# Self-attention of sixteen short sequences: scores three pairs ahead, and half of the last rotation behind the first division

## The chip, the core and the metric

The kernel runs on one core of a Trainium2 chip. The metric is the device time of one execution in microseconds (us). Its engines have names of their own in the profile: PE is TensorE (matrix products; PEld its weight loads), DVE is VectorE, ACT is ScalarE, POOL is GpSimd, SP is SyncE, which issues the transfers. Each engine takes its instructions in the order of the program and waits at semaphores for the others.

## What is computed

Four transformer-like blocks in a row over x (16 sequences of 56 tokens, 256 features) with a context of 1500 tokens per sequence. The change touches only the self-attention at the start of the first block:

```
x = rms_norm(hidden_states, ln_in_w)
mixed = jnp.where(vm, x @ v_qkv, x @ l_qkv)
q, k, v = jnp.split(mixed, 3, axis=-1)
q, k, v = (heads(q, NH, HD), heads(k, NH, HD), heads(v, NH, HD))
q, k = apply_rotary(q, k, position_ids, l)
ctx = sdpa(q, k, v, causal=True)          # 16 heads of 16 features, 56 x 56 scores, softmax
ctx = ctx.transpose(0, 2, 1, 3).reshape(b, l, H)
attn_out = jnp.where(vm, ctx @ v_dense, ctx @ l_dense)
hidden_states = residual + attn_out
```

`apply_rotary` gives `q * cos + rotate_half(q) * sin`, and the same for k. Behind it stand the cross-attentions and feed-forward layers, which take over 90% of the time and are the same in both kernels.

## The kernel before

Features lie on the partitions, the 896 tokens along the free axis, in two halves of 448 (`half(h)`), that is 8 sequences each. `R` holds q, k and v as six tiles `qkv[:, m]` of 128 features: m = 0, 1 are q, 2, 3 are k, 4, 5 are v.

**Rotation.** For each half and each of the four tiles of q and k (in the order `TURNED` = 2, 3, 0, 1), TensorE makes the turned copy (`turn`, one product with a constant), and VectorE's `rotate(h, m)` does three instructions of 448 columns: the sine product out of PSUM into XN (L1359), which also frees the PSUM bank; the cosine product in place (L1360); their sum in place (L1362), which raises the semaphore `rotated`. The last two tiles of the second half (m = 0, 1: its q) are rotated in the middle of the first pair, ahead of the first division.

**Pairs.** Self-attention works on two sequences at a time, a pair i of `HB` = 8. Nearly all tiles are there twice and are taken in turns (`i % 2`). For a pair:

- staging: ScalarE's `sa_stage` spreads v (L909, two instructions) and q (L912); GpSimd's `stage_keys` makes k masked by head (L697, four products);
- TensorE `sa_scores`: in two banks the causal mask (L1877) and q times k (L1879);
- VectorE `sa_maximum` (L1371) and `sa_shift`, which subtracts the maximum out of PSUM (L1377);
- ScalarE `sa_exps` (L917);
- VectorE `sa_total` (the sum L1382, its reciprocal L1385) and `sa_divide` (L1389), which gives the probabilities;
- TensorE `sa_turned`: eight transposes of the probabilities into banks 1 and 2 (line 1902 in the rows); ScalarE `sa_turned` copies them to SBUF (L937, two instructions);
- TensorE `sa_values`: v transposed into bank 0 (L1891 in the rows); ScalarE `sa_values` copies it out (L927, two);
- TensorE `sa_attended`: probabilities times values into bank 3 (L1916); ScalarE `sa_attended` copies the result to XN (L944).

Each engine's order is written out by hand as a loop over i. TensorE runs attended(i-1), values(i+1), scores(i+2), turned(i). ScalarE runs stage(i+2), attended(i-1), values(i+1), exps(i+1), turned(i). VectorE runs maximum(i+1), total(i), shift(i+1), divide(i). GpSimd makes the keys of pair i as soon as scores(i-2) are done. Keys of pair 4 and later also wait until the second half's k is rotated, and the staging of pair 4 until all of `rotated` is there. Behind the last pair follow the split of XN by expert on VectorE (L1273, L1276) and the dense product on TensorE (L1810).

Of the kernel before, what the change touches and what calls it, by code (L numbers as in the profile page):

```python
# [40 lines left out]
HT = T // 2  # L41
# [157 lines left out]
def build(nc, a, out):  # L199

    ctx = ExitStack()
    with ctx:
# [648 lines left out]
        def _(act):  # L851
# [97 lines left out]
            sa_stage(1)  # L949
            sa_exps(0)  # L950
            sa_values(0)
            for i in range(HB):
                if i + 2 < HB:
                    sa_stage(i + 2)
                if i > 0:
                    sa_attended(i - 1)
                if i + 1 < HB:
                    sa_values(i + 1)
                    sa_exps(i + 1)
                sa_turned(i)  # L960
            sa_attended(HB - 1)

# [257 lines left out]
        def _(dve):  # L1220
# [131 lines left out]
            def rotate(h, m):  # L1352

                src = take(dve, ("turn", h, m))
                if turns[0] > 0:
                    dve.wait_ge(sem("rotated"), turns[0])
                turns[0] += 1
                other, own = XN[:, m % 2, half(h)], qkv[:, m, half(h)]
                inc_empty(V.tensor_tensor(by_seq(other), by_seq(src[:, 0:HT]), bs(sinT), ALU.mult))  # L1359
                then(V.tensor_tensor(by_seq(own), by_seq(own), bs(cosT), ALU.mult))  # L1360
                emptied(dve, ("turn", h, m))
                V.tensor_tensor(own, own, other, ALU.add).then_inc(sem("rotated"), 1)  # L1362
# [28 lines left out]
            for name, m in SECOND_HALF:  # L1391
# [4 lines left out]
                if name == "turn":  # L1396
                    rotate(0, m)
                else:
                    leave(1, m)
# [12 lines left out]
            for m in TURNED[0:2]:  # L1412
                rotate(1, m)
            for i in range(HB):
                if i + 1 < HB:
# [4 lines left out]
                if i == 0:  # L1420
                    for m in TURNED[2:4]:
                        rotate(1, m)
                sa_divide(i)
            for h in range(2):
                dve.wait_ge(sem("sa_out"), HB // 2 * (h + 1))
                by_expert("experts2", h)
# [368 lines left out]
        def _(pe):  # L1795
# [138 lines left out]
            for m in TURNED[2:4]:  # L1934
                turn(1, m)
            sa_values(0)
            for i in range(HB):
                if i > 0:
                    sa_attended(i - 1)
                if i + 1 < HB:  # L1940
                    sa_values(i + 1)
                if i + 2 < HB:
                    sa_scores(i + 2)
                sa_turned(i)
            sa_attended(HB - 1)

# [586 lines left out]
```

## Time and profile before

| | |
|---|---|
| time, median of 3 runs | 1597.53 us (1596.61 to 1602.24) |
| the profiled execution, its own time | 1597.96 us |
| its span in the profile | 1596.2 us |
| mean granted TensorE clock | 0.98 of full |
| TensorE busy | 1476.0 us, 92% of the span |
| VectorE busy | 945.8 us, 59% |
| ScalarE busy | 621.8 us, 39% |
| GpSimd busy | 539.6 us, 34% |
| DMA engines, hardware queue | 17.7% of 16 engines' span |

The span goes from the first to the last instruction; the execution's own time has 1.8 us around it. Busy shares are averages over very different stages. Self-attention of the pairs lies between about 66 and 120 us. A timeline row gives start, duration, engine, line, operation, what is written and read, how often it stands in a row, and in square brackets how long the engine was idle before it and who ended that.

### The profile page before, as it was taken

The numbers are of one execution on the slowest core, as the hardware profiler recorded it, in microseconds if no ns is written. First come the engines' busy times: TensorE is split into PE (matmuls) and PEld (weight loads), VectorE is DVE, ScalarE is ACT, GpSimd is POOL, SyncE is SP. The second block draws the span as 40 slices with busy tenths as digits, with TensorE's granted clock in tenths as the row PEclk, the third lists the DMA queues.
The fourth block names the chain that finished last, engine by engine and source line by source line (L and its number), as shares of the span: only waits on it lengthen the run. The fifth ranks groups of instructions, "written<-read, shape, count | busy, mean of one in ns | idle before, by whom it ended". The sixth has DMA issues, their size and how long they took to land.

```text
span 1596.2 us, 21925 instructions
## 1 busy us (share of the span) xinstructions
PE 1476.0 (92%) x8042; PEld 781.9 (49%) x8043; DVE 945.8 (59%) x1605; ACT 621.8 (39%) x1014; POOL 539.6 (34%) x425
## 2 busy tenths in 40 slices
PE   6779999999999899989988899999999889999898
PEld 3346555555555444446654344455344344555344
DVE  6877666666666264114437677777333768778440
ACT  1253466666666520035542233334122333333131
POOL 1620488888888910000001133332000133333000
PEclk9989999999999999989999999999999989999999
DMA  7001532232331140023212001110031001110000
GB/s 253 0 2 36 136 97 71 76 98 64 84 80 50 27 138 0 0 78 106 88 34 64 0 25 43 40 36 1 2 112 65 0 21 40 36 36 13 2 0 23
DMA packets 42276, 82.96 MB, mean 52 GB/s; under 512 B 6252, under 2 KB 28188, under 8 KB 42156
## 3 DMA queue, kind: packets, MB, share of 16 engines
q1 hardware_dynamic: 42160, 81.48, 17.7%
q8 instruction: 65, 1.06, 0.3%
q14 instruction: 51, 0.42, 0.1%
HBM read 59.31 MB, written 0.97 MB: 38 GB/s over the span
## 4 chain that ended last, share of the span: by engine, by line
PE 79%; DVE 12%; POOL 3%; ACT 2%; issue 2%; DMA 0%; SPq 0%; POOLq 0%; ACTq 0%; DVEq 0%
PE psum L1810 21%; PE psum L2393 8%; PE psum L2051 5%; PE psum L2027 5%; PE psum L2001 3%; PE psum L2334 3%; DVE WBZ L1713 3%; PE psum L1984 3%; PE psum L2201 3%; PE psum L1970 2%; POOL XN L780 2%; PE psum L2365 2%; DVE WA L1453 2%; PE psum L2401 2%; PE psum L2385 2%
## 5 line engine op out<-in xcount | busy, mean ns | idle before, releaser
L1453 DVE TENSOR_REDUCE WA<-psum 112x2 f32<-112x1000 f32 x192 | 229.8, 1201 | 89.9 <-PE psum L2001 89.9
L780 POOL TENSOR_TENSOR XN<-XN,WBZ 125x896 f32<-125x896 f32 x128 | 266.5, 2082 | 16.8 <-POOL XN L780 0.9
L1172 ACT ACTIVATE WA<-psum,y_bias 125x448 f32<-125x448 f32 x192 | 121.1, 633 | 227.7 <-PE psum L2388 226.7
L1006 ACT ACTIVATE WBZ<-psum 125x896 f32<-125x896 f32 x192 | 175.5, 915 | 43.9 <-PE psum L2027 33.3
L2393 PE MATMUL psum<-WA,ctxN 125*128 125x448 f32 x384 | 179.8, 552 | 0.4 <-ACT WA L1172 0.4
L812 POOL TENSOR_TENSOR XN<-const,y_max 112x896 bf16<-112x896 f32 x32 | 53.7, 1679 | 309.6 <-DVE y_max L1700 237.4
L1700 DVE CUSTOM_DVE_ANT_0 XA<-psum,WA 112x375 bf16<-112x375 f32 x240 | 122.7, 540 | 35.9 <-PE psum L2365 35.9
L803 POOL TENSOR_SCALAR ctxT<-ctxT 128x375 f32<-128x375 f32 x32 | 56.1, 1754 | 190.3 <-ACT std L881 187.8
L2027 PE MATMUL psum<-R 100*125 100x224 f16 x768 | 110.6, 266 | 0.0
L1713 DVE RECIPROCAL WBZ<-WBZ 128x224 f32<-128x224 f32 x68 | 105.2, 1549 | 1.2
L2365 PE MATMUL psum<-XB,R 128*112 128x375 f16 x240 | 77.7, 344 | 22.7 <-DVE y_max L1700 22.7
L2027 PEld LDWEIGHTS psum<-R 100*125 100x125 f16 x768 | 78.9, 135 | 28.3 <-issue 25.0
L1810 PE MATMUL psum<-R,WBZ 128*128 128x448 f32 x224 | 88.5, 548 | 2.5 <-ACT R L886 2.5
L2393 PEld LDWEIGHTS psum<-WA,ctxN 125*128 125x128 f32 x384 | 67.3, 191 | 31.7 <-ACT WA L1172 24.4
L2001 PE MATMUL psum<-WA,XB 32*112 32x500 f16 x384 | 79.3, 413 | 2.5 <-DVE WA L1453 2.3
L1810 PE MATMUL psum<-XA,WA 64*128 64x448 f32 (+1 forms) x216 | 72.5, 573 | 2.1 <-DVE XA L1634 2.0
L2385 PE MATMUL psum<-R,XB 128*125 128x448 f16 x192 | 68.7, 358 | 4.9 <-POOL XN L812 4.9
L2365 PEld LDWEIGHTS psum<-XB,R 128*112 128x112 f16 x240 | 31.6, 131 | 84.3 <-DVE y_max L1700 69.5
L2388 PE MATMUL psum<-XN,minusb 112*125 112x448 bf16 x192 | 68.9, 359 | 0.0
L2387 PE MATMUL psum<-R,XB 128*125 128x448 f16 x192 | 68.5, 357 | 0.0
L2386 PE MATMUL psum<-R,XB 128*125 128x448 f16 x192 | 68.4, 356 | 0.0
L1810 PEld LDWEIGHTS psum<-R,WBZ 128*128 128x128 f32 x224 | 40.9, 189 | 50.1 <-issue 44.7
(266 smaller groups left out, 2567.4 us busy)
## 6 DMA issues: line engine op xcount, KB each, us to landing
R<-WA SPq DMA_DIRECT2D x192, 93.8 KB, 2.2
ctxT<-in_ctxT SPq DMA_DIRECT2D x12, 750.0 KB, 4.2
R<-in_ctxT SPq DMA_DIRECT2D x12, 750.0 KB, 5.4
WA<-in_ctxT SPq DMA_DIRECT2D x8, 750.0 KB, 4.2
ctxT<-in_ctxT SPq DMA_DIRECT2D x32, 187.5 KB
ctxN<-in_ctx SPq DMA_DIRECT2D x32, 187.5 KB
WBZ<-in_x_w SPq DMA_DIRECT2D x4, 1024.0 KB, 6.3
WA<-bias_rows SPq DMA_DIRECT2D x30, 82.0 KB, 3.8
```

The lines of the kernel that those rows point to most:

```text
L780: nc.gpsimd.tensor_tensor(z_sum[b % 2][0:TK, :], first[0:TK, :], z_p[t % 4][0:TK, :], ALU.add)\
L1006: nc.scalar.activation(z_p[t % 4][0:TK, :].rearrange("p (k n) -> p k n", k=2), psum[0:TK, s:s + 2, 0:2 * GC], ACT.Exp, scale=float(CHD0) * ...
L1172: nc.scalar.activation(y_pT[t][0:TK, g * HALF:(g + 1) * HALF], bank[2 + u % 3][0:TK, 0:HALF], ACT.Exp, bias=y_bias[0:TK, bass.ds(b * NT + ...
L1453: V.tensor_reduce(z_mx[0:PR, r:r + 3:2, c], psum[0:PR, lo:lo + 2, 0:PC], AX_X, ALU.max)\
L1700: V.tensor_tensor_reduce(y_masked[0:PR, j % 2, 0:CK], bank[j % 2][0:PR, 0:CK], y_mask[0:PR, s, 0:CK], 1.0, -3e38, ALU.add, ALU.max, y_max[ ...
L1713: V.reciprocal(part, part).then_inc(sem("x2_inverted"), 1)
L1810: mm = pe.matmul(bank[bk][0:w.shape[-1], 0:HT], w, m, start=(i == 0), stop=(i == len(parts) - 1))
L2001: mm = pe.matmul(bank[lo + j][0:PR, 0:PC], z_dh[at, b, 2 * (i % 2):2 * (i % 2) + 2, :].rearrange("p h s -> p (h s)"), z_kh[b % 2][at, c * ...
L2027: mm = pe.matmul(bank[2 * (t % 2) + g // 2][0:TK, g % 2 * GC:(g % 2 + 1) * GC], KS[0:KR, b % 2, g, t * TK:(t + 1) * TK], QS[0:KR, g, b, :] ...
L2365: return pe.matmul(bank[j % 2][0:PR, 0:CK], y_q[:, b, 0, j * PR:(j + 1) * PR], y_k[:, s, 0, 0:CK], start=True, stop=True)
L2385: pe.matmul(dst, y_k[:, s, 0, at], q[0], start=True, stop=False)
L2393: return pe.matmul(bank[5 + g][:, 0:HALF], ctxN[s][0:TK, t, :], y_pT[t][0:TK, g * HALF:(g + 1) * HALF], start=(t == 0), stop=(t == KT - 1))
```

## The change

Three of the hand-written orders change; no instruction is added or removed.

- TensorE: scores run three pairs ahead instead of two, and stand between turned(i) and attended(i). values(i+2) follow attended(i). Scores of pair 2 stand ahead of values of pair 1.
- ScalarE: the loop is values(i+1), turned(i), exps(i+2), attended(i), stage(i+4); staging of pairs 2 and 3 and the exponential of pair 1 stand ahead of the loop.
- VectorE: `rotate` is cut in two. The sine product stays in it, the cosine product and the sum are `rotated`. For the last two tiles `rotated` comes behind the division of pair 0. The wait of the sine product on the semaphore `rotated` asks for one less.

```diff
             sa_stage(0)
             sa_stage(1)
             sa_exps(0)
+            sa_stage(2)
             sa_values(0)
+            sa_exps(1)
+            sa_stage(3)
             for i in range(HB):
-                if i + 2 < HB:
-                    sa_stage(i + 2)
-                if i > 0:
-                    sa_attended(i - 1)
                 if i + 1 < HB:
                     sa_values(i + 1)
-                    sa_exps(i + 1)
                 sa_turned(i)
-            sa_attended(HB - 1)
+                if i + 2 < HB:
+                    sa_exps(i + 2)
+                sa_attended(i)
+                if i + 4 < HB:
+                    sa_stage(i + 4)
...
             def rotate(h, m):
 
                 src = take(dve, ("turn", h, m))
-                if turns[0] > 0:
-                    dve.wait_ge(sem("rotated"), turns[0])
+                if turns[0] > 1:
+                    dve.wait_ge(sem("rotated"), turns[0] - 1)
                 turns[0] += 1
+                other = XN[:, m % 2, half(h)]
+                inc_empty(V.tensor_tensor(by_seq(other), by_seq(src[:, 0:HT]), bs(sinT), ALU.mult))
+
+            def rotated(h, m):
                 other, own = XN[:, m % 2, half(h)], qkv[:, m, half(h)]
-                inc_empty(V.tensor_tensor(by_seq(other), by_seq(src[:, 0:HT]), bs(sinT), ALU.mult))
                 then(V.tensor_tensor(by_seq(own), by_seq(own), bs(cosT), ALU.mult))
                 emptied(dve, ("turn", h, m))
                 V.tensor_tensor(own, own, other, ALU.add).then_inc(sem("rotated"), 1)
...
                     for m in TURNED[2:4]:
                         rotate(1, m)
                 sa_divide(i)
+                if i == 0:
+                    for m in TURNED[2:4]:
+                        rotated(1, m)
...
             sa_values(0)
+            sa_scores(2)
+            sa_values(1)
             for i in range(HB):
-                if i > 0:
-                    sa_attended(i - 1)
-                if i + 1 < HB:
-                    sa_values(i + 1)
+                sa_turned(i)
+                if i + 3 < HB:
+                    sa_scores(i + 3)
+                sa_attended(i)
                 if i + 2 < HB:
-                    sa_scores(i + 2)
-                sa_turned(i)
-            sa_attended(HB - 1)
+                    sa_values(i + 2)
```

The lines of the changed kernel are shifted: on VectorE by up to 5, on TensorE by 10.

TensorE in the middle of the pairs, before: L1902 are the turned probabilities, L1916 attended values, L1891 values, L1877 and L1879 scores.

```order
L1902 MATMUL psum<-const,WBZ 128x128 x8
L1916 MATMUL psum<-WBZ 32x56 x16
L1891 MATMUL psum<-const,R 128x128 x4
L1877 MATMUL psum<-probs 128x448
L1879 MATMUL psum<-R 64x448 x2
L1877 MATMUL psum<-probs 128x448
L1879 MATMUL psum<-R 64x448 x2
L1902 MATMUL psum<-const,R 128x128 x8
```

The same place after, where L1912, L1926, L1901, L1887 and L1889 are those lines.

```order
L1912 MATMUL psum<-const,R 128x128 x8
L1887 MATMUL psum<-probs 128x448
L1889 MATMUL psum<-R 64x448 x2
L1887 MATMUL psum<-probs 128x448
L1889 MATMUL psum<-R 64x448 x2
L1926 MATMUL psum<-R 32x56 x16
L1901 MATMUL psum<-const,R 128x128 x4
L1912 MATMUL psum<-const,WBZ 128x128 x8
```

The scores moved from behind attended and values to between turned and attended.

VectorE from the subtraction of pair 1 to the maximum of pair 2, before: L1359, L1360 and L1362 are the rotation, L1389 is the division.

```order
L1377 TENSOR_TENSOR WBZ<-psum,small 128x16x56
L1359 TENSOR_TENSOR XN<-psum,sinT 128x448
L1360 TENSOR_TENSOR R<-R,cosT 128x448
L1362 TENSOR_TENSOR R<-R,XN 128x448
L1359 TENSOR_TENSOR XN<-psum,sinT 128x448
L1360 TENSOR_TENSOR R<-R,cosT 128x448
L1362 TENSOR_TENSOR R<-R,XN 128x448
L1389 TENSOR_TENSOR R<-R,nmax 128x16x56
L1371 TENSOR_REDUCE small<-psum 128x16
```

And after, where L1361, L1365, L1367 and L1394 are those lines.

```order
L1382 TENSOR_TENSOR WBZ<-psum,small 128x16x56
L1361 TENSOR_TENSOR XN<-psum,sinT 128x448 x2
L1394 TENSOR_TENSOR R<-R,nmax 128x16x56
L1365 TENSOR_TENSOR R<-R,cosT 128x448
L1367 TENSOR_TENSOR R<-R,XN 128x448
L1365 TENSOR_TENSOR R<-R,cosT 128x448
L1367 TENSOR_TENSOR R<-R,XN 128x448
L1376 TENSOR_REDUCE small<-psum 128x16
```

The division stands four instructions earlier; the maximum of pair 2 has the same work ahead of it.

ScalarE in the loop, after: L927 values, L937 the copy of the turned probabilities, L917 the exponential of the pair after next, L944 attended, L909 and L912 staging. Before, L937 was followed at once by L909 and L912 of the pair after next, and L917 was the last ahead of L937.

```order
L927 ACTIVATE R<-psum 64x16x16 x2
L937 ACTIVATE WBZ<-psum 128x512 x2
L917 ACTIVATE WBZ<-WBZ 128x16x56
L944 ACTIVATE XN<-psum 128x2x112
L909 ACTIVATE R<-R 128x2x2x56 x2
L912 ACTIVATE R<-R 128x2x2x56
```

The staging moved behind the exponential and the attended values.

## Rows read from the trace of the kernel before

**Rows 1.** The page: TensorE's busy time, and the chain by engine.

```profile
PE 1476.0 (92%) x8042; PEld 781.9 (49%) x8043; DVE 945.8 (59%) x1605; ACT 621.8 (39%) x1014; POOL 539.6 (34%) x425
...
PE 79%; DVE 12%; POOL 3%; ACT 2%; issue 2%; DMA 0%; SPq 0%; POOLq 0%; ACTq 0%; DVEq 0%
```

**Rows 2.** TensorE's timeline, 66 to 85 us: start, duration, engine, line, operation.

```profile
68.92 0.35 PE L1877 MATMUL psum<-probs 128*128 128x448 bf16 x1 [0.36 <-issue]
...
70.40 0.97 PE L1879 MATMUL psum<-R 128*64 128x448 f32 x4
76.33 1.97 PE L1902 MATMUL psum<-const,R 128*128 128x128 f32 x8 [4.96 <-DVE R L1389]
```

**Rows 3.** TensorE's timeline over one pair, 84.9 to 92 us.

```profile
84.97 1.09 PE L1902 MATMUL psum<-const,WBZ 128*128 128x128 f32 x8
87.24 0.60 PE L1916 MATMUL psum<-WBZ 128*32 128x56 f32 x32 [1.17 <-ACT WBZ L937]
...
90.65 1.09 PE L1902 MATMUL psum<-const,R 128*128 128x128 f32 x8
```

**Rows 4.** VectorE's timeline, 52 to 137 us.

```profile
70.18 0.61 DVE L1359 TENSOR_TENSOR XN<-psum,sinT 128x448 f32<-128x448 f32 x1
70.71 0.62 DVE L1360 TENSOR_TENSOR R<-R,cosT 128x448 f32<-128x448 f32 x1
...
73.30 1.24 DVE L1362 TENSOR_TENSOR R<-R,XN 128x448 f32<-128x448 f32 x1
74.46 1.82 DVE L1389 TENSOR_TENSOR R<-R,nmax 128x896 f32<-128x896 f32 x1
76.20 1.08 DVE L1371 TENSOR_REDUCE small<-psum 128x16 f32<-128x896 f32 x1
...
79.73 1.08 DVE L1389 TENSOR_TENSOR WBZ<-WBZ,nmax 128x896 f32<-128x896 f32 x1
85.09 1.09 DVE L1371 TENSOR_REDUCE small<-psum 128x16 f32<-128x896 f32 x1 [4.28 <-PE psum L1879]
```

**Rows 5.** GpSimd's timeline: two products of pair 4, four of pair 5.

```profile
71.53 1.25 POOL L697 TENSOR_TENSOR R<-R,const 128x448 f32<-128x448 f32 x1 [2.22 <-PE psum L1879]
...
74.02 1.31 POOL L697 TENSOR_TENSOR R<-R,const 128x448 f32<-128x448 f32 x1
...
85.14 3.62 POOL L697 TENSOR_TENSOR R<-R,const 128x448 f32<-128x448 f32 x4 [8.06 <-PE psum L1879]
```

**Rows 6.** ScalarE's timeline, 84.9 to 92 us.

```profile
86.10 1.08 ACT L937 ACTIVATE WBZ<-psum 128x512 f32<-128x512 f32 x2 [2.83 <-PE psum L1902]
87.07 0.67 ACT L909 ACTIVATE R<-R 128x224 f32<-128x224 f32 x2
87.63 0.39 ACT L912 ACTIVATE R<-R 128x224 f32<-128x224 f32 x1
```

**Rows 7.** Stretches: us, PE, PEld, DVE, ACT, POOL busy, clock, DMA, GB/s.

```profile
80.00:84.20 4.20, 4.20 (x32) 1.71 (x26) 0.81 (x1) 2.32 (x5) 0.00 (x0) 0.50 0.02 4
...
90.00:95.70 5.70, 4.53 (x56) 2.28 (x54) 4.52 (x5) 3.90 (x10) 3.62 (x4) 1.00 0.00 1
...
111.50:114.90 3.40, 1.26 (x20) 1.02 (x24) 2.80 (x4) 2.46 (x5) 0.00 (x0) 1.00 0.00 0
```

**Rows 8.** TensorE's timeline, 107 to 124 us: the tail, the dense products.

```profile
107.67 1.09 PE L1902 MATMUL psum<-const,WBZ 128*128 128x128 f32 x8
...
112.47 1.09 PE L1902 MATMUL psum<-const,R 128*128 128x128 f32 x8 [1.34 <-DVE R L1389]
...
115.53 1.97 PE L1902 MATMUL psum<-const,WBZ 128*128 128x128 f32 x8
118.68 0.97 PE L1916 MATMUL psum<-WBZ 128*32 128x56 f32 x32 [1.17 <-ACT WBZ L937]
119.58 2.83 PE L1810 MATMUL psum<-XA,WA 128*128 128x448 f32 x4
122.25 1.67 PE L1810 MATMUL psum<-XB,WA 128*128 128x448 f32 x4
```

More of the change, by code:

```diff
@@ L1397, in _ @@
                     rotate(0, m)
+                    rotated(0, m)
                 else:
@@ L1423, in _ @@
                 sa_divide(i)
+                if i == 0:
+                    for m in TURNED[2:4]:
+                        rotated(1, m)
             for h in range(2):
```

## The prediction

> **What bounds the kernel now.** The page first: TensorE is busy 92% of the span, and 79% of the chain that ended last runs through it, so time is won only where TensorE waits [rows 1]. The change touches self-attention alone, about 66 to 120 us. There I read TensorE's timeline for its gaps, then the other engines' for what fills them. Three kinds of gap show. One of 4.96 us before the first turned probabilities (76.33) ends with VectorE's first division [rows 2]. In every pair, 1.18 us pass between turned probabilities and attended values, while ScalarE copies the transposes out of PSUM: 84.97 + 1.09 = 86.06 to 87.24 [rows 3]. And a tail: pairs 6 and 7 have nothing to put in between [rows 8]. A pair costs 90.65 - 84.97 = 5.68 us, which is turned 1.09, the gap 1.18, and 3.41 for attended, values and scores (87.24 to 90.65) [rows 3]. VectorE needs 79.73 + 1.08 - 76.20 = 4.61 us for a pair [rows 4], and it idles for TensorE's scores (4.28 us before 85.09) [rows 4]. So TensorE's own order sets the pace.
>
> **Part 1, the start.** Row 68.92: scores of pair 2 wait for ScalarE's staging, which stood behind a 0.77 us copy of values; now it stands ahead of it. They start at about 68.1 and end at 70.6 instead of 71.4 [rows 2]. GpSimd's four key products, released by them, start at 70.7 instead of 71.53 [rows 5]. VectorE issues the two sine products at 70.18 and 70.71 (0.53 us is the spacing of the first two of rows 4) and reaches the first division at 71.25. There is contention in the rows: an instruction of 448 elements that reads two SBUF tensors takes 0.62 us alone (70.71) and 1.24 beside GpSimd's product (73.30), the division 1.08 alone (79.73) and 1.82 beside it (74.46), and GpSimd's product, 0.9 alone (four in 3.62), goes to 1.31 [rows 4, 5]. The division now waits until GpSimd's first product ends at 71.65 and ends itself at 72.65. **Turned probabilities of pair 0 start at 72.7 instead of 76.33**, 3.6 us earlier.
>
> **Part 2, what the early division leaves late.** The four other rotation instructions (cosine product and sum, twice) come behind it. They run beside GpSimd's remaining three products and the first of the next four. Row 73.30 to row 74.46 is 1.16 us for such an instruction under contention. Low bound: no contention, 4 x 0.58 = 2.3 us. High bound: all four contended and in line with their predecessors, 4 x 1.25 = 5.0. I take 4 x 1.2 = 4.8, since each meets a product in progress. So the maximum of pair 2 starts at 72.65 + 4.8 = 77.5 instead of 76.20, and the division of pair 1 ends at 77.5 + 4.61 = 82.1. **Turned probabilities of pair 1 start at 82.15 instead of 84.97**, 2.8 us earlier: 0.8 of the 3.6 is lost here again.
>
> The Trainium skill, SBUF - State Buffer, section "SBUF: two separate sides", has a rule that speaks against this part: a VectorE instruction with two SBUF inputs and a GpSimd one that reads SBUF lock each other out for a whole instruction. By that rule alone five VectorE instructions (the division, four of the rotation) would each stand behind up to one full product, 5 x 0.9 = 4.5 us at most, where the rows give what I use, 0.4 + 2.5 = 2.9; the sum would be up to 1.6 us longer. The trace agrees in kind: the measured excess is 0.6 and 0.7 us.
>
> **Part 3, the clock.** TensorE now runs turned 0, scores 3, attended 0 and values 2 from 72.7: 1.09 + 3.41 = 4.5 us, to 77.2; the copy between is covered. Then it has nothing until 82.15, 4.95 us. In a gap of 4.96 us before, the granted clock went to half (1.2 of 2.4 GHz), and it came back at 84.2, 7.9 us after TensorE resumed; the last 4.2 of them were without a pause [rows 2, 7]. I expect the fall again. How long it lasts after 82.15 is bounded by 4.2 (no pause now, the scores fill the copy's gap) and 7.9; I take 5.5, near the lower end for that reason. Half clock for 5.5 us costs 2.75 us of work. **Turned 2 starts at 82.15 + 4.5 + 2.75 = 89.4** instead of 90.65.
>
> **Part 4, the steady pairs.** The copy's gap is gone: turned, scores, attended, values make 5.68 - 1.18 = 4.5 us. Who is late next? VectorE, 4.61, but it is ahead of TensorE after part 3. ScalarE: busy 3.9 us in a pair [rows 7]. Its queue has one new wait: the exponential of pair i+2 stands before the staging of pair i+4 and waits for VectorE's subtraction. Staging takes 1.0 us (87.07 to 87.63 + 0.39) [rows 6] from the end of values on TensorE, which turned (1.09) just covers; so scores are held by 0.1 us at most. The copies themselves, 1.08, now lie beside scores of 2.4. GpSimd's 3.6 us per pair lies beside all of it [rows 5]. Turned 3, 4, 5: 89.4 + 3 x 4.5 = **102.9 instead of 107.67** [rows 8].
>
> **Part 5, the tail.** VectorE's maximum of pair 4 waits for scores 4, which end at 82.15 + 1.09 + 2.4 + 2.75 = 88.4 (2.4 for scores is 68.92 to 70.40 + 0.97 in rows 2). From there four pairs of 4.61 bring the division of pair 6 to 106.8, later than TensorE is free: 102.9 + 2.27 for turned and the bare copy, + 1.0 for attended and values (3.41 less 2.4), is 106.2. Turned 6 at 106.85 instead of 112.47. Then nothing covers the copies: attended 6 at 109.1, turned 7 at 109.7, attended 7 at 111.95, and the **dense product starts at 112.5 instead of 119.58** [rows 8]: 7.1 us. Before, the clock was at half there, and the first dense product took 2.83 us instead of 1.67 [rows 8], 1.16 more. If the clock is up there now, this comes on top.
>
> **Sum.** 7.1 + 1.1 = 8.2 us. Behind it everything follows at a fixed distance: TensorE runs without pause from 119.58 on, and the chain of the whole span has no transfer in it (DMA 0% in rows 1). The profiled execution took 1597.96 us (span 1596.2), 0.4 over the median, so 1589.8 for its like and 1597.53 - 8.2 = **1589.3** for the median.
>
> **Rivals.** *(a) The clock falls in the tail as well.* For: it fell before turned 7, where TensorE had worked 1.26 us between 111.5 and 114.9 [rows 7]; the bare copies of the tail stay. Against: the gap of 1.34 us before turned 6 [rows 8], where TensorE waited for VectorE, shrinks to 0.7, so the tail is denser. Price: what it cost before, turned 7 with 1.97 instead of 1.09, attended 7 with 0.97 instead of 0.60, and 1.16 in the dense product, 2.4 in all: 5.8 us, **1591.7**.
>
> *(b) The start is better.* The clock holds, or GpSimd's products don't meet the rotation. Without the low clock VectorE sets the pace: division 6 ends at 82.1 + 5 x 4.61 = 105.2, 1.6 us earlier: **1587.7**; without contention as well, 2.5 more: 1585.2. For: nothing but that a gap's place against the clock's changes may differ. Against: both showed in the rows of before.
>
> *(c) ScalarE's new wait binds.* If its exponential holds back the staging in each steady pair by 0.5 us, four pairs make 2 us: **1591.3**. Against: 3.9 us of work in 4.5, so ScalarE has 0.6 to spare.
>
> *(d) The head start is given back* at the first start of the cross-attention, by a load or by GpSimd: **1597.5**. Against: the two contexts and the weights are loaded from the start of the program, and what waits for the last attended values (two loads of SyncE's queue) has the whole dense stage beside it.
>
> *(e) Slower than before: the clock stays low.* With a gap of 5 us and then a tail, TensorE could stay at 1.2 GHz through all pairs. A pair then costs 9.0 us instead of 5.68; turned 5 at 82.15 + 4 x 9.0 = 118.2 instead of 107.67, 10.5 later, about 1 more behind it: **1609**. It decides from the point where the low stretch lasts 16 us more than I assume (16 / 2 = 8 us, the whole gain). Against: it came back each time that TensorE had work without pause.
>
> **How the numbers follow.** The forecast 0.40, (a) 0.25, (b) 0.17, (c) 0.08, (d) 0.04, (e) 0.06. The size of the forecast's own unknowns (contention 2.3 to 5.0, low clock 4.2 to 7.9 us) is worth from -3.1 (2.5 and half of 1.3) to +1.4 us (0.2 and half of 2.4). A measurement of this kernel tells about 0.5% from no change, 8.0 us, 1589.5: the forecast stands right on it. Of its own 0.40 I count 0.23 beyond 0.5%, of (a) and (c) 0.05, of (b) all: faster 0.45, within 0.5% 0.49, slower 0.06. The range reaches from the better half of (b) to beyond (a) and (c): 1586 to 1594.5; left out are (d), (e) and the best of (b).
>
> **What would show it.** Right: turned 0 near 72.7, a gap of 5 us before turned 1 near 82, half clock for 4 to 8 us behind it, then 4.5 us between turned probabilities, no wait of TensorE for the PSUM copy in pairs 0 to 4, and the dense product at 112.5 with 1.67 us. Wrong: turned 1 before 80 (no contention), pairs of 5 us or more with TensorE waiting for ScalarE's staging (c), or a wait at the start of the cross-attention that was not there (d).

## The result, and the profile after

The changed kernel took **1591.19 us** (median of 6 runs, 1590.39 to 1592.23) against 1601.12 of the kernel before (median of 6, 1596.61 to 1602.24). The ratio is 0.9945 with a 95% interval of 0.993 to 0.9959 (the two medians alone would give 0.9938): faster, by about half a percent. The profiled executions went from 1597.96 to 1590.39, their spans from 1596.2 to 1588.6 us. The kernel before does not always take the same time: its runs beside the experiments lie near 1597, near 1602 and near 1612 to 1617 us, each group at a lower mean clock (0.980, 0.975, 0.967), and what probably makes the highest group is shown under "Rotated later". Profiles are therefore compared here by the stretch of this one stage.

The page of the kernel after: busy times, and shares of the chain that ended last by engine.

```profile
PE 1473.9 (93%) x8042; PEld 780.1 (49%) x8043; DVE 946.9 (60%) x1605; ACT 621.6 (39%) x1014; POOL 539.5 (34%) x425
...
PE 79%; DVE 13%; POOL 3%; issue 2%; ACT 2%; DMA 0%; SPq 0%; POOLq 0%; ACTq 0%; DVEq 0%
```

Nothing changed in what bounds the kernel; only idle time of TensorE went. Its timeline after (start, duration, engine, line, operation, operands, idle before), to be laid beside [rows 2, 3, 8]. L1912 are the turned probabilities of pairs 0, 1, 2, 3, 5, 6 and 7, L1887 the first scores of pair 5, L1926 the last attended values, L1820 the dense product:

```profile
72.15 1.09 PE L1912 MATMUL psum<-const,R 128*128 128x128 f32 x8 [1.51 <-DVE R L1394]
...
81.79 1.97 PE L1912 MATMUL psum<-const,WBZ 128*128 128x128 f32 x8 [5.14 <-DVE WBZ L1394]
...
88.67 1.04 PE L1912 MATMUL psum<-const,R 128*128 128x128 f32 x8
89.92 0.35 PE L1887 MATMUL psum<-probs 128*128 128x448 bf16 x1 [0.21 <-issue]
...
93.33 1.04 PE L1912 MATMUL psum<-const,WBZ 128*128 128x128 f32 x8
...
102.64 1.04 PE L1912 MATMUL psum<-const,WBZ 128*128 128x128 f32 x8
...
106.41 1.09 PE L1912 MATMUL psum<-const,R 128*128 128x128 f32 x8 [0.38 <-DVE R L1394]
...
109.21 1.09 PE L1912 MATMUL psum<-const,WBZ 128*128 128x128 f32 x8
111.48 0.98 PE L1926 MATMUL psum<-WBZ 128*32 128x56 f32 x32 [1.18 <-ACT WBZ L937]
112.38 2.86 PE L1820 MATMUL psum<-XA,WA 128*128 128x448 f32 x4
```

The gap of 4.96 us before turned 0 [rows 2] is 1.51 now, and one of 5.14 stands before turned 1. Pairs follow at 4.66 us (88.67 to 93.33) instead of 5.68 [rows 3]. The dense product starts at 112.38 instead of 119.58 [rows 8], and takes 2.86 us as it took 2.83: it lies at half clock again. Stretches of the same kernel, with the granted clock (PEclk) to be compared with [rows 7]:

```profile
core 0: us, PE busy (x) PEld busy (x) DVE busy (x) ACT busy (x) POOL busy (x), PEclk, DMA share, GB/s
...
80.50:87.30 6.80, 5.51 (x18) 2.40 (x18) 5.66 (x7) 4.71 (x10) 0.00 (x0) 0.50 0.00 0
...
111.20:114.60 3.40, 3.12 (x35) 1.93 (x36) 1.66 (x3) 0.58 (x2) 0.00 (x0) 0.50 0.28 47
```

**Where the 7.6 us of the span are.** TensorE reaches this stage a little earlier or later in every execution, for reasons ahead of the change. So I count from the start of the last turned copy of q and k (one group of four products, 64.84 before, 64.31 after), called *offset* from here on:

```profile
64.84 1.77 PE L1810 MATMUL psum<-R,const 128*128 128x448 f32 x4
```
```profile
64.31 1.77 PE L1820 MATMUL psum<-R,const 128*128 128x448 f32 x4
```

The kernel after was 0.53 earlier there by chance. Turned 2 came at an offset of 24.36 instead of 25.81: 1.45 gained. From turned 2 to the dense product it took 23.71 instead of 28.93: 5.22 gained. The dense product's offset is thus 48.07 instead of 54.74, 6.67 less, and that of the end of its first four products 50.93 instead of 57.57. The other 0.4 lies in all the rest of the span. Of the 7.6 us, then, 6.6 to 6.7 are the change's in this pair of profiles, and 1.0 is chance.

### The profile page after: what moved, and what is told of

The parts are those of the page before. It is cut to its first block, busy times and chain, and to the rows that moved or that the text cites. A ratio compares the mean times of both kernels' runs of the same rounds, so it can differ in the third digit from the quotient of the medians.

```text
span 1588.6 us, 21924 instructions
## 1 busy us (share of the span) xinstructions
PE 1473.9 (93%) x8042; PEld 780.1 (49%) x8043; DVE 946.9 (60%) x1605; ACT 621.6 (39%) x1014; POOL 539.5 (34%) x425
## 4 chain that ended last, share of the span: by engine, by line
PE 79%; DVE 13%; POOL 3%; issue 2%; ACT 2%; DMA 0%; SPq 0%; POOLq 0%; ACTq 0%; DVEq 0%
PE psum L1820 21%; PE psum L2403 8%; PE psum L2061 5%; PE psum L2037 5%; PE psum L2011 4%; PE psum L2344 3%; DVE WBZ L1723 3%; PE psum L1994 3%; PE psum L2211 3%; PE psum L1980 2%; POOL XN L780 2%; PE psum L2375 2%; DVE WA L1463 2%; PE psum L2411 2%; PE psum L2395 2%
## 5 line engine op out<-in xcount | busy, mean ns | idle before, releaser
L1820 PE MATMUL psum<-R,WBZ 128*128 128x448 f32 x224 | 88.5, 548 | 2.5 <-ACT R L886 2.5
L1820 PE MATMUL psum<-XA,WA 64*128 64x448 f32 (+1 forms) x216 | 72.5, 573 | 2.1 <-DVE XA L1644 1.9
L1820 PEld LDWEIGHTS psum<-R,WBZ 128*128 128x128 f32 x224 | 40.9, 189 | 50.1 <-issue 44.7
```

What stands on the lines that cost most here:

```text
L1820: mm = pe.matmul(bank[bk][0:w.shape[-1], 0:HT], w, m, start=(i == 0), stop=(i == len(parts) - 1))
```

## The experiments

Each kernel is given as a difference from the changed kernel. "Dense" is the dense product's offset, "first product" that of the end of its first four products; before 54.74 and 57.57, after 48.07 and 50.93. Times without an interval are one execution each. A ratio is taken against the runs of the kernel before that were made beside the kernel in question. The share of its high runs differs between these sets (above 1611 us: 0 of 6, 5 of 18, 6 of 19 and 1 of 19), and for the same changed kernel the ratio is 0.9945 in one set and 0.9906 in another; so ratios of different sets should not be compared closely. All offsets are of one profile each, and where the half clock falls differs between profiles of one kernel: the changed kernel, profiled again (below), has 46.68 and 48.45. Differences of some 2.5 us in the stage can be due to that.

**Orders only.** The whole rotation stands ahead of the division again; the orders of TensorE and ScalarE are the changed ones.

```diff
                     for m in TURNED[2:4]:
                         rotate(1, m)
+                        rotated(1, m)
                 sa_divide(i)
-                if i == 0:
-                    for m in TURNED[2:4]:
-                        rotated(1, m)
```

> The new orders of TensorE and ScalarE, with VectorE's rotation whole and ahead of the first division as before. My theory is that the start is worth little, because what the early division wins is lost to the contention with GpSimd, the gap before the second turned probabilities and the low clock behind it, and that the gain comes from the pairs: turned 0 at about 76, no gap before turned 1 (which starts at about 83, TensorE being the late one), turned 5 at about 102 and the dense product at 112 to 113 as in the changed kernel (112.4), so about 8 us less than the kernel before. The rival: the 3.6 us at the start are kept, so that without them the dense product starts at about 116 and the gain is 4 to 5 us.

Measured 1591.54 us (9 runs, 1583.03 to 1604.3), ratio 0.9923 (0.9876 to 0.9969); dense 46.81, first product 48.58: in the stage this is 1.3 us less than the first profile of the full change and 0.1 more than its second, so the split shows no gain of its own here. TensorE's rows, turned 0, 1, 2 and the dense product:

```profile
77.07 1.97 PE L1910 MATMUL psum<-const,R 128*128 128x128 f32 x8 [5.58 <-DVE R L1394]
...
83.91 1.04 PE L1910 MATMUL psum<-const,WBZ 128*128 128x128 f32 x8
...
88.63 1.04 PE L1910 MATMUL psum<-const,R 128*128 128x128 f32 x8
...
111.96 1.77 PE L1818 MATMUL psum<-XA,WA 128*128 128x448 f32 x4
```

By offset turned 0 is 4.1 us later than after (11.92 against 7.84), and the gap of 5.6 stands before it. But the half clock (75.7 to 82.5) then lies under turned 0 and scores 3, VectorE's division 1 is done meanwhile (at 81.54, where turned 1 starts at 83.91), and turned 1 waits for nothing. Turned 2 is at an offset of 23.48, 0.9 ahead of the first profile of the full change (24.36) and 0.1 behind its second (23.35). The split only moves the gap, and the half clock with it, from before turned 0 to before turned 1.

**Vector only.** The split rotation alone; TensorE's and ScalarE's loops are those of before. Only TensorE's part of the edit is shown.

```diff
...
             sa_values(0)
-            sa_scores(2)
-            sa_values(1)
             for i in range(HB):
-                sa_turned(i)
-                if i + 3 < HB:
-                    sa_scores(i + 3)
-                sa_attended(i)
-                if i + 2 < HB:
-                    sa_values(i + 2)
+                if i > 0:
+                    sa_attended(i - 1)
+                if i + 1 < HB:
+                    sa_values(i + 1)
+                if i + 2 < HB:
+                    sa_scores(i + 2)
+                sa_turned(i)
+            sa_attended(HB - 1)
...
```

> Only VectorE's part of the change: half of the last rotation behind the first division, the orders of TensorE and ScalarE as before. My theory: turned 0 at about 72.5, turned 1 at about 82 after a gap of about 4 us, then 5.7 us per pair as before; 0 to 3 us less than the kernel before, depending on whether the clock falls in that gap. The rival (the start is the gain): 3.5 us less or more.

Measured 1600.5 us, ratio 0.9988 (0.9959 to 1.0018): no difference. Dense 55.92, 1.2 later than before. Turned 1 and 2:

```profile
82.42 1.97 PE L1910 MATMUL psum<-const,WBZ 128*128 128x128 f32 x8 [2.93 <-DVE WBZ L1392]
...
91.71 1.09 PE L1910 MATMUL psum<-const,R 128*128 128x128 f32 x8
```

Turned 1 is 2.5 us earlier than at 84.97 [rows 3], as predicted; but half clock lasts from 81.4 to 91.6, and turned 2 is later than 90.65. Here the head start was lost to the clock that fell behind it.

**TensorE's order alone**, with ScalarE's loop and the rotation of before. Only ScalarE's loop is shown.

```diff
...
+                if i + 2 < HB:
+                    sa_stage(i + 2)
+                if i > 0:
+                    sa_attended(i - 1)
                 if i + 1 < HB:
                     sa_values(i + 1)
+                    sa_exps(i + 1)
                 sa_turned(i)
-                if i + 2 < HB:
-                    sa_exps(i + 2)
-                sa_attended(i)
-                if i + 4 < HB:
-                    sa_stage(i + 4)
+            sa_attended(HB - 1)
...
```

> Only TensorE's order of the change, ScalarE's and VectorE's as before. Scores of the third pair ahead then wait for their staging, which stands behind the copy of the turned probabilities on ScalarE: a pair should take 1.1 + 1.1 + 1.0 + 2.4 + 0.5 + 0.5 = 6.6 us instead of 5.7, and the kernel be 3 to 4 us slower than before. If TensorE's order were enough, a pair would take 4.5 to 4.7 us as in the changed kernel.

Measured 1632.13 us, dense 70.91, far more than the 3 to 4 us that I expected. Turned 1, first scores of pair 4, turned 2:

```profile
85.51 1.04 PE L1908 MATMUL psum<-const,WBZ 128*128 128x128 f32 x8
89.49 0.35 PE L1883 MATMUL psum<-probs 128*128 128x448 bf16 x1 [2.95 <-issue]
...
92.90 1.04 PE L1908 MATMUL psum<-const,R 128*128 128x128 f32 x8
```

Scores wait 2.95 us in each pair for a staging that stands behind the copy of the turned probabilities on ScalarE. A pair takes 7.39 us, and with a wait of that length in each the clock fell again and again: pairs of 8.9 and 10.1 follow. The stage is 16.2 us longer than before (70.91 against 54.74). The rest of the loss lies in the cross-attention, where half clock lasted 41 us with TensorE busy almost all the time (compare "Rotated later"):

```profile
190.30:231.30 41.00, 40.61 (x216) 20.73 (x214) 16.63 (x16) 14.55 (x18) 18.67 (x9) 0.50 0.30 80
```

TensorE's new order is a loss without ScalarE's; ScalarE's alone was not run.

**Keys late.** GpSimd's first key products of the second half wait for the whole rotation, so nothing of it runs beside the division.

```diff
-                    pool.wait_ge(sem("rotated"), 2 * KD * h + 2)
+                    pool.wait_ge(sem("rotated"), 2 * KD * h + (4 if h else 2))
```

> The changed kernel, but GpSimd's key products of pair 4 wait until all rotations are done, so they don't run beside them. If contention costs what I put down, the division takes 1.08 instead of 1.58 us, the four instructions behind it 2.4 instead of 5.1, turned 1 starts at about 79 instead of 81.8, and the gap before it is about 2 us, so that the clock may stay up; the dense product then starts at about 108 (clock up) or 109.5 (clock down). If contention does not matter, turned 1 stays at 81.8 and the dense product at 112.4, or comes later because the keys do.

Measured 1588.15 us, dense 45.26. VectorE and GpSimd in the kernel after (division 0, the first of the four rotation instructions, maximum 2; the first four key products):

```profile
70.51 1.58 DVE L1394 TENSOR_TENSOR R<-R,nmax 128x896 f32<-128x896 f32 x1
72.02 1.35 DVE L1365 TENSOR_TENSOR R<-R,cosT 128x448 f32<-128x448 f32 x1
...
77.12 1.08 DVE L1376 TENSOR_REDUCE small<-psum 128x16 f32<-128x896 f32 x1
```
```profile
70.21 5.23 POOL L697 TENSOR_TENSOR R<-R,const 128x448 f32<-128x448 f32 x4 [1.63 <-PE psum L1889]
```

and with the keys late, VectorE, then TensorE's turned 1:

```profile
71.22 1.08 DVE L1394 TENSOR_TENSOR R<-R,nmax 128x896 f32<-128x896 f32 x1
72.22 0.62 DVE L1365 TENSOR_TENSOR R<-R,cosT 128x448 f32<-128x448 f32 x1
...
74.61 1.08 DVE L1376 TENSOR_REDUCE small<-psum 128x16 f32<-128x896 f32 x1
```
```profile
79.40 1.97 PE L1912 MATMUL psum<-const,WBZ 128*128 128x128 f32 x8 [2.53 <-DVE WBZ L1394]
```

Division and rotation take 3.39 us instead of 6.61, so the contention costs VectorE 3.2. GpSimd's four products, 3.62 when undisturbed [rows 5], take 5.23 beside the division and the rotation. The gap before turned 1 halves to 2.53, yet the clock fell all the same (half from 78.7 to 85.5).

**q first.** ScalarE's staging of pair i+4 is cut in two: q ahead of the copy of the attended values, v behind it. Scores need only q; `sa_values` waits for v on a semaphore of its own. Only ScalarE's loop is shown.

```diff
...
+                if i + 4 < HB:
+                    sa_stage_q(i + 4)
                 sa_attended(i)
                 if i + 4 < HB:
-                    sa_stage(i + 4)
+                    sa_stage_v(i + 4)
...
```

> The changed kernel, but ScalarE stages q of the fourth pair ahead before it copies the attended values, with a semaphore of its own for v. In the changed kernel TensorE waits 0.21 us before the scores of each steady pair; if that is the staging of q, the wait goes and a pair takes 4.45 to 4.55 us instead of 4.66, and the dense product starts about 0.5 us earlier. If it is something else (GpSimd's keys, or the loads of weights), a pair stays at 4.66.

Measured 1589.84 us, dense 47.69. After, ScalarE's v (L909) and q (L912) end at 89.82, just ahead of the scores at 89.92:

```profile
88.87 0.67 ACT L909 ACTIVATE R<-R 128x224 f32<-128x224 f32 x2 [0.20 <-PE psum L1901]
89.45 0.37 ACT L912 ACTIVATE R<-R 128x224 f32<-128x224 f32 x1
```

With q first, turned 3, scores of pair 6, turned 4, turned 6:

```profile
92.67 1.04 PE L1935 MATMUL psum<-const,WBZ 128*128 128x128 f32 x8
93.54 0.35 PE L1909 MATMUL psum<-probs 128*128 128x448 bf16 x1
...
96.94 1.04 PE L1935 MATMUL psum<-const,R 128*128 128x128 f32 x8
...
105.76 1.09 PE L1935 MATMUL psum<-const,R 128*128 128x128 f32 x8 [1.08 <-DVE R L1416]
```

Scores start 0.87 behind turned instead of 1.25, and the pair takes 4.27. But VectorE's pace is next: turned 6 now waits 1.08 for its division instead of 0.38, and of 3 x 0.37 only 0.4 is left.

**Filled gap.** Sixteen products of constants into a free bank, 128 x 224, whose result nobody reads, stand in the gap before turned 1.

```diff
                 if i + 2 < HB:
                     sa_values(i + 2)
+                if i == 0:
+                    pe.wait_ge(sem("sa_pT"), 1)
+                    for _ in range(16):
+                        pe.matmul(bank[1][:, 0:224], mean, const[:, 0:224], start=True, stop=True)
```

> The changed kernel with 16 products without use in TensorE's gap before the turned probabilities of pair 1, so that the clock has no reason to fall there; about 4.3 us of work in a gap of 5.1. If the low clock is what makes TensorE late in pairs 1 and 2, the granted clock stays at full, turned 2 starts at about 86.4 instead of 88.7, and the dense product at about 110.5 instead of 112.4. If the clock costs nothing there, the dense product stays at 112.4.

Measured 1593.05 us, dense 46.21, 1.9 less than after; the first product ends only 1.4 earlier, as half clock came in the tail (110.1 to 116.9). The fillers and turned 1:

```profile
77.56 6.22 PE L1959 MATMUL psum<-const 128*128 128x224 f32 x32
83.62 1.04 PE L1912 MATMUL psum<-const,WBZ 128*128 128x128 f32 x8
```

They took 0.38 us each, more than the 0.27 I had counted, and delayed turned 1 by 0.8 (offset 18.23 against 17.48). Even so turned 2 came 1.85 earlier (22.51 against 24.36): the clock stayed up, and turned 1 took 1.04 instead of 1.97. That is the price of those 6.8 us of half clock by itself, 1.85 + 0.75 = 2.6 us.

**Rotated later.** The four rotation instructions stand behind the *second* division.

```diff
                 sa_divide(i)
-                if i == 0:
+                if i == 1:
                     for m in TURNED[2:4]:
                         rotated(1, m)
```

> The changed kernel with the four rotation instructions behind the division of pair 1 instead of pair 0. Turned 1 should start at about 77.3 instead of 81.8 and the gap before it go; scores of pair 4 then wait for the rotated q, to about 82.5. If the rotation's place is what costs, the maximum of pair 4 comes at about 85 instead of 87.8 and the dense product at about 110; if the wait only moves, the dense product stays at 112.

Measured 1605.63 us, with dense at 47.23, 0.8 *less* than after. Turned 1 and the first scores of pair 4:

```profile
77.04 1.09 PE L1912 MATMUL psum<-const,WBZ 128*128 128x128 f32 x8
82.61 0.53 PE L1887 MATMUL psum<-probs 128*128 128x448 bf16 x1 [4.48 <-POOL R L697]
```

The wait only moves: scores of pair 4 need keys and q of the second half. The extra 15 us are elsewhere, in the cross-attention, where half clock lasts from 166.9 to 204.4. The stretch from 166 to 204 us, first in this kernel, then in the run of the changed kernel again (below):

```profile
166.00:204.00 38.00, 37.36 (x202) 19.58 (x198) 16.07 (x16) 13.97 (x17) 18.67 (x9) 0.51 0.30 77
```
```profile
166.00:204.00 38.00, 36.61 (x350) 20.52 (x348) 25.81 (x25) 23.02 (x31) 31.90 (x19) 1.00 0.51 134
```

TensorE is busy 98% of the time, at half clock, and the view counts 202 of its instructions instead of 350. The mean clock of this execution is 0.970, and the highest times of the other kernels, the one before too, come with clocks of 0.965 to 0.971; so I take them for the same thing. No high run of the kernel before was profiled, so for that kernel it is not shown, and neither is what makes its middle group near 1602.

**All together, split rotation.** Keys late, q first, six fillers before turned 1, and three before each of the last two attended values. Only the fillers of the tail are shown.

```diff
...
                 sa_turned(i)
                 if i + 3 < HB:
                     sa_scores(i + 3)
+                if i > 5:
+                    pe.wait_ge(sem("sa_shifted"), HB)
+                    for _ in range(3):
+                        pe.matmul(bank[4][:, 0:224], mean, const[:, 0:224], start=True, stop=True)
                 sa_attended(i)
...
```

> The changed kernel with GpSimd's products of pair 4 behind the rotations, q staged ahead of the attended values' copy, six products without use in the gap before turned 1 and three in each of the two bare copies of the tail. If the three costs found add up (contention 2.8 us, low clock in the pairs 2, low clock in the tail 1.7), the clock stays at full from 65 to 130 us, VectorE sets the pace at 4.55 us a pair, turned 1 starts 14.4 us after the last turn product as in the kernel with late keys, and the first dense product ends about 44.5 us after it, where the changed kernel has 50.9: 5 to 6.5 us less than the changed kernel. If VectorE or something else takes over, less than 3 us.

Dense 42.65, first product 44.42: 6.5 less than in the first profile of the changed kernel, 4.0 less than in its second. Turned 1 and 2 and the dense product:

```profile
80.13 1.09 PE L1935 MATMUL psum<-const,WBZ 128*128 128x128 f32 x8 [0.26 <-DVE WBZ L1416]
...
84.67 1.09 PE L1935 MATMUL psum<-const,R 128*128 128x128 f32 x8
...
108.40 1.77 PE L1842 MATMUL psum<-XA,WA 128*128 128x448 f32 x4
```

The clock stays up throughout the stage, and VectorE sets the pace of 4.53. Against the first profile the costs found one at a time add up in the stage. The time doesn't show it: 1590.35 (12 runs), ratio 0.9922 (0.9885 to 0.9959). Four of the twelve runs, the profiled one among them, lie at 1603.3 to 1604.6: here half clock lasted from 161.7 to 199.2 us. The other eight have a median of 1589.4, against 1589.72 of the changed kernel in the same set.

**All together, whole rotation.** The same with the rotation of before, whole and ahead of the division, and ten fillers behind values 1 instead of the six. Only these are shown.

```diff
...
             sa_scores(2)
             sa_values(1)
+            emptied(pe, ("turn", 1, 0))
+            for _ in range(10):
+                pe.matmul(bank[1][:, 0:224], mean, const[:, 0:224], start=True, stop=True)
...
```

> The same with the rotation whole and ahead of the first division, as in the kernel before, and the products without use in the gap ahead of turned 0. If VectorE's part of the change is worth nothing, this one is within 0.5 us of the kernel with everything (turned 0 at 3 us later, turned 1 at 0.3 us later). If the early division is worth something once clock and contention are out of the way, this one is 1 us or more slower.

Measured **1584.11 us** (6 runs, 1583.13 to 1586.82), ratio 0.9866 (0.9823 to 0.9909): the best kernel of the study, and in the same set none of its runs is as slow as the fastest of the changed kernel (1588.86). Dense 43.89, first product 45.66. The fillers, turned 0, turned 1, and turned 6:

```profile
70.03 3.95 PE L1972 MATMUL psum<-const 128*128 128x224 f32 x20
73.82 1.04 PE L1933 MATMUL psum<-const,R 128*128 128x128 f32 x8
...
78.14 1.09 PE L1933 MATMUL psum<-const,WBZ 128*128 128x128 f32 x8
...
100.81 1.97 PE L1933 MATMUL psum<-const,R 128*128 128x128 f32 x8 [1.08 <-DVE R L1416]
```

With the keys late and TensorE kept at work, the whole rotation costs nothing up to the tail: turned 1 is at an offset of 14.27, where the split kernel had 14.38. In this profile the clock was at half for 3.4 us in the tail (100.4 to 103.8), under turned 6, and that is what makes dense 1.2 later than in the split kernel. Behind the first product the span is 1475.5 us long, against 1473.4 and 1473.9 in the two profiles of the changed kernel: some 1.6 to 2.1 us of what the stage gained are lost again further on. There is half clock from 527.1 to 533.9 here, which those two don't have.

**The changed kernel again**, beside the two above.

> The changed kernel again, beside the two others on the same chip: 0.993 to 0.996 of the kernel before, as measured first. In the trace, if no 35 to 40 us stretch of low clock shows in the cross-attention, the span is near 1588.6 us.

Measured 1589.72 us (8 runs), ratio 0.9906 (0.9872 to 0.9939). The last turned copy, turned 1, turned 2 and the dense product:

```profile
65.49 1.77 PE L1820 MATMUL psum<-R,const 128*128 128x448 f32 x4
...
82.96 1.97 PE L1912 MATMUL psum<-const,WBZ 128*128 128x128 f32 x8 [5.14 <-DVE WBZ L1394]
...
88.84 1.04 PE L1912 MATMUL psum<-const,R 128*128 128x128 f32 x8
...
112.17 1.77 PE L1820 MATMUL psum<-XA,WA 128*128 128x448 f32 x4
```

The same instructions give dense 46.68 and first product 48.45, 1.4 and 2.5 less than in the first profile: half clock lasted 3.4 us behind turned 1 (82.8 to 86.2) instead of 6.8 and didn't come in the tail, where the dense product's first row is 1.77 and not 2.86.

**Without fillers, whole rotation**: keys late and q first alone, the rotation of before.

```diff
...
                     for m in TURNED[2:4]:
                         rotate(1, m)
+                        rotated(1, m)
                 sa_divide(i)
-                if i == 0:
-                    for m in TURNED[2:4]:
-                        rotated(1, m)
...
```

> The orders of TensorE and ScalarE of the change, VectorE's rotation whole as before, GpSimd's products of pair 4 behind the rotations, q staged ahead; no products without use. If those only keep the clock up and cost nothing else, the gap before turned 0 (about 4 us) brings a low clock of 3.4 or 6.8 us, and the dense product starts 45 to 46.5 us after the last turn product (43.9 with them): 1.5 to 2.5 us slower than that kernel, 1586 to 1587 in executions without the long low stretch in the cross-attention. If the filling has a cost of its own further on, as the times of the kernel with everything (1589 without the long stretch) may mean, this one is as fast as it or faster.

Measured 1590.52 us (10 runs), ratio 0.9943 (0.9915 to 0.9972); dense 45.39, first product 48.46. TensorE waits 3.41 us before turned 0, and half clock came there for 3.4 us and in the tail for 10.2.

**Without fillers, split rotation**: the same two, the rotation as changed.

> The same with the rotation split as in the changed kernel. A gap of about 2.5 us before turned 1; with a low clock there the dense product starts about 45 us after the last turn product, as in the kernel with late keys (45.3) less 0.3. If the early division is worth nothing, the time is within 1 us of the kernel with the whole rotation.

Measured 1588.85 us (10 runs, of which one took 2877.33 us; no trace shows why, and the ratio leaves it out), ratio 0.9928 (0.9904 to 0.9952); dense 45.03, first product 47.99, half clock for 10.2 us in the tail. Here too split and whole rotation differ by less than can be told (0.4 us in the stage; the intervals overlap). Beside the two kernels with everything, 48.46 and 47.99 stand against 45.66 and 44.42: in the stage of these profiles the fillers are worth 2.8 and 3.6 us, by keeping the clock up. In the whole span they are worth less: behind the first product the two kernels without fillers have 1473.7 and 1473.8 us, and the one with fillers and whole rotation has 1475.5. In time (medians of all runs) the four are at 1584.1 against 1590.5 us (whole) and 1590.4 (1589.4 without its high runs) against 1588.9 (split), in two different sets of runs.

## Why the prediction was right, point by point

The forecast was 8.2 us, a ratio of 0.9949; measured were 0.9945 and 7.6 us between the two spans. The mechanism was right: turned 0 early, a gap and half clock before turned 1, then pairs without the copy's gap. As offsets, forecast and measured are 17.31 and 17.48 for turned 1, 24.56 and 24.36 for turned 2, 38.06 and 38.33 for turned 5, 47.66 and 48.07 for the dense product, 49.33 and 50.93 for the end of its first four products. Two errors cancel in the middle: from turned 1 to turned 2 I had 7.25 us where it took 6.88, and for the next three pairs 13.5 where they took 13.97.

The closeness of the totals is partly luck. The change itself gave 6.6 us at the end of the first product, 1.6 less than forecast: attended 7 at half clock cost 0.4 of that and the first dense product 1.2. The 1.0 us of chance outside the stage makes it 7.6. The time, 1591.19, lies nearer to rival (a)'s 1591.7 than to my 1589.3. And the ratio is near 0.9949 also because the kernel before came out higher in its later runs (median 1601.12 of six, where I had 1597.53 of three). The second profile of the changed kernel gained 9.1 us at the end of the first product, 0.9 more than forecast.

- **Part 1, right.** Turned 0 at 72.15 for 72.7, and 0.53 of that difference is the chance lead at the start of the stage. The contended division took 1.51 us from its start to the next (70.51 to 72.02), within the 1.0 and 1.8 that [rows 4] gave.
- **Part 2, right as a mechanism, a little short.** The four rotation instructions took 5.10 us (72.02 to 77.12) for the 4.8 taken and a high bound of 5.0. The excess of division and rotation over the kernel with late keys is 3.2 us, where I had 2.9 from the rows and, as an estimate, up to 4.5 by the lock rule of the Trainium skill (SBUF - State Buffer, "SBUF: two separate sides"). The trace agrees with the rule in kind and lies nearer to the price from the rows. Turned 1 came at 81.79 for 82.15, by offset 0.17 late.
- **Part 3, right.** A gap of 5.14 for 4.95, the clock at half behind it, for 5.5 us after TensorE resumed (81.79 to 87.3), as taken. The size is no constant, though: 3.4 us in all when the same kernel was run again.
- **Part 4, the mis-sized term.** A pair takes 4.66 us, not 4.5, and I had it wrong twice. I added the duration of turned, 1.09, where the next product starts 0.87 behind it: without a wait a pair is 4.27 ("q first"). And I let turned cover the staging but for 0.1 us, where scores are held by 0.38. ScalarE starts v 0.20 behind the start of turned (88.67 to 88.87), its staging takes 0.95, and TensorE resumes 0.10 behind the end of q's (89.82 to 89.92): the two small delays I left out. The rule of rival (c), then, that staging holds the scores, is true in each pair, at 0.38 us and not 0.5; but q first won only 0.4 us in all, since VectorE (4.53 for a pair, I had 4.61) is right behind.
- **Part 5, start right, clock wrong.** Turned 6 at 106.41 for 106.85, waiting for VectorE as said, and the dense product at 112.38 for 112.5. The 1.1 us from the first dense product did not come: half clock fell on it, as in rival (a), but it began only at 111.2, so of (a)'s 2.4 us the 0.9 under turned 7 is missing (1.09, as at full clock), while attended 7 (0.98) and the product (2.86) have theirs. It was 0.25 against 0.40 in my chances. The second profile of the same kernel had the clock up there, so executions of one kernel differ in it, and the forecast should have carried that as a spread of some 2.5 us in the stage.
- **What cause the gain has.** Here the text was wrong, though the sum was not hurt. Parts 1 to 3 read as if turned 1 came 2.8 us earlier thanks to the split, and 1.25 of it were left at turned 2. "Orders only" reaches turned 2 at an offset of 23.48 without the split, where the full change has 24.36 and 23.35, and the split alone gives a ratio of 0.9988. All of the gain that is shown is the two loops'. I never asked what the orders would do with the rotation left whole. In that case the gap of 5.6 us comes before turned 0 and not before turned 1, and the half clock behind it makes turned 1 2.4 us later than its division; either way the stage pays for one long gap and one stretch of half clock.
- **(b)**: not in the first profile, where both the contention and 6.8 us of half clock came. In the second the half clock was shorter, 3.4 us, so a part of (b) came there.
- **(d)**: no. The stretch from TensorE's first products on the maxima of the cross-attention (below, before and after) to the end of the span is as long in both kernels, 1431.3 and 1430.9, so nothing was given back.

```profile
164.89 0.55 PE L2014 MATMUL psum<-const,WA 112*4 112x112 f32 x4 [1.42 <-DVE WA L1461]
```
```profile
157.72 0.55 PE L2024 MATMUL psum<-const,WA 112*4 112x112 f32 x4 [1.42 <-DVE WA L1471]
```

- **(e)**: not in this kernel; "TensorE's order alone" shows that the clock can fall again and again once each pair has a wait of 3 us. What I held against it, that the clock came back each time that TensorE had work without pause, does not hold in general: in three profiles it stayed at half for 37.5 to 41 us with TensorE busy 98 or 99% of the time.

**What stays open.** Whether "orders only" differs in time from the full change: 0.9923 (0.9876 to 0.9969) and 0.9945 (0.993 to 0.9959) overlap, and they come from different sets. What ScalarE's order would do alone. Why the kernel with everything and the split rotation, in the stage 4.0 us ahead of the changed kernel profiled beside it, is at 1589.4 in its undisturbed runs against 1589.7, while its sister with the whole rotation, 2.8 ahead, is at 1584.1: only one execution of each has a trace, and the first one's is a disturbed one. And what ends or begins the long stretch of half clock.

## What to carry to other kernels

When two changes travel together, ask for each what the other would do alone: an order that hides a wait can absorb the very gap that the second edit removes. A chain's length is the distance between starts, not a sum of durations, and here a hand-over between TensorE and ScalarE cost 0.1 to 0.2 us in each direction that no instruction's row shows. Moving a wait is not removing it: whole and split rotation end within 0.4 us of each other without fillers (45.39 and 45.03). And profile one kernel twice before reading a difference of 1 or 2 us between two: here the same instructions differed by 2.5.

## What the runs showed of the hardware

- Half clock can last 37.5 to 41 us with TensorE busy for 98 or 99% of the time (166.9 to 204.4, 161.7 to 199.2 and 190.3 to 231.3 us in "rotated later", "all together, split rotation" and "TensorE's order alone", clock 0.50), against stretches of 3.4 to 13.7 us in and just behind self-attention. Executions with it take some 15 us more. Times that fit it are 4 of 12 in "all together, split rotation", 2 of 9 in "orders only" and 12 of 56 of the kernel before in the sets beside the experiments; that these all have it is concluded from their mean clock, as only three such executions, of changed kernels, were profiled.
- A pause of 2.5 us can be enough for the fall (2.53 and 2.54 us in "keys late" and in the last kernel: it came in the first and not in the second). So the length of a gap alone doesn't decide.
- VectorE's products of two SBUF operands and GpSimd's slow each other down: 448 columns go from 0.62 to 1.24 and 1.35 us, 896 from 1.08 to 1.58, GpSimd's from 0.9 to 1.3. Holding GpSimd back gives VectorE 3.2 us, and in the one profile of it the stage is 2.8 and 1.4 us shorter than in the two profiles of the changed kernel.
- A product of float32 constants 128 x 224 takes 0.38 us in two passes at full clock (16 in 6.06 us).
